# Graph passes with one comparison per group for the one-hots, and the edge weight applied on ScalarE

## What is computed

```python
# layer 0, per head; p = exp(leaky_relu(a_src[src] + a_dst[dst]) - max)
out = segment_sum(p[:, :, None] * h[src], dst)       # 256 columns + 4 of p
# layer 2
messages = edge_val[:, None] * embeddings[edge_src]
neighbor_emb = segment_sum(messages, edge_dst)       # 256 columns
```

## Time and profile before

| | |
|---|---|
| median of 3 runs | 9505.01 us (9503.06 to 9507.33) |
| profiled execution, first to last instruction | 9491.7 us |
| first graph pass, in the span | 187 to 2396 us |
| second graph pass, in the span | 3767 to 5880 us |
| busy: PE, DVE, ACT, POOL | 71%, 57%, 10%, 62% |
| mean granted clock of TensorE | 0.83 of full speed |

### The profile page before, as it was taken

How to read it: one execution, slowest core, us unless ns; L and a number is a source line. 1 busy time by engine, 2 the same in 40 slices (tenths; PEclk the granted TensorE clock), 3 DMA queues, 4 the chain that set the end, 5 groups by cost and what they waited for, 6 DMA issues and landing times. The chain is left out here.

```text
span 9491.7 us, 113426 instructions
## 1 busy us (share of the span) xinstructions
PE 6725.8 (71%) x23837; PEld 4472.8 (47%) x23838; DVE 5384.8 (57%) x13915; ACT 978.0 (10%) x2770; POOL 5926.5 (62%) x6521
## 2 busy tenths in 40 slices
PE   4777777777389992555555555677777777777893
PEld 3666666666256661444444444533333333333562
DVE  4777777777641114555555555566666666666422
ACT  1111111111033330000000000200000000000331
POOL 3777777777011115777777775077777777777125
PEclk7888888888599996777777777689999999999896
DMA  3333333333310003333333332100000000000113
GB/s 110 102 101 101 101 101 101 101 101 101 97 59 30 31 30 108 104 104 104 104 104 104 104 104 80 28 5 5 5 5 5 5 5 5 5 5 5 61 58 101
DMA packets 348160, 613.47 MB, mean 65 GB/s; under 512 B 123719, under 2 KB 223627, under 8 KB 348094
## 3 DMA queue, kind: packets, MB, share of 16 engines
q0 software_dynamic: 237632, 507.28, 21.1%
q1 hardware_dynamic: 110462, 105.48, 3.5%
HBM read 550.01 MB, written 62.36 MB: 65 GB/s over the span
## 5 line engine op out<-in xcount | busy, mean ns | idle before, releaser
L622 POOL DMA_INDIRECT g_G<-table,g_STG x3328 | 3254.4, 978 | 956.3 <-issue 887.7
L776 PE MATMUL g_pM<-g_G,g_S 128*128 128x260 f32 (+1 forms) x6656 | 2358.0, 519 | 1061.0 <-DMA g_G<-table,g_STG 1056.7
L776 PEld LDWEIGHTS g_pM<-g_G,g_S 128*128 128x128 f32 x6656 | 1665.5, 263 | 1575.0 <-issue 1112.0
L1355 PE MATMUL q_pS<-q_MV,q_OL 128*128 128x500 f32 (+1 forms) x4096 | 1966.7, 632 | 596.7 <-DVE q_MV L1251 596.7
L658 DVE TENSOR_TENSOR acc<-g_pM,acc 128x260 f32 (+1 forms) x3328 | 1407.5, 423 | 780.1 <-PE g_pM L776 757.8
L1355 PEld LDWEIGHTS q_pS<-q_MV,q_OL 128*128 128x128 f32 x4096 | 817.8, 207 | 1506.2 <-issue 841.0
L1162 POOL DMA_INDIRECT q_G<-table,q_STG x1024 | 1107.9, 1082 | 293.3 <-issue 293.3
L1251 DVE TENSOR_TENSOR q_MV<-q_OH,q_V 128x980 f32<-128x980 f32 x1024 | 1169.7, 1173 | 153.0 <-PE q_pS L1355 137.5
L1165 POOL DMA_INDIRECT q_A<-adst,q_STG x768 | 944.4, 1230 | 234.0 <-issue 233.4
L1690 POOL DMA_INDIRECT e_XI<-rows,e_STG x206 | 200.2, 972 | 1089.2 <-PE e_pI L1762 1086.0
L649 DVE TENSOR_SCALAR g_S<-iota,g_REL,g_WT 128x128 f32<-128x128 f32 x1664 | 617.9, 372 | 194.9 <-issue 178.3
(11 more groups left out here) (257 smaller groups left out, 4622.3 us busy)
## 6 DMA issues: line engine op xcount, KB each, us to landing
g_G<-table,g_STG POOLq DMA_INDIRECT x3328
ys<-e_Y SPq DMA_DIRECT2D x206, 128.0 KB, 1.7
ew_W<-in_L_ffn_W SPq DMA_DIRECT2D x16, 1024.0 KB, 9.2
q_G<-table,q_STG POOLq DMA_INDIRECT x1024
rows<-t_XR SPq DMA_DIRECT2D x98, 128.0 KB, 1.7
q_A<-adst,q_STG POOLq DMA_INDIRECT x768
table<-p_OUT SPq DMA_DIRECT2D x49, 130.0 KB, 1.9
f_H<-table SPq DMA_DIRECT2D x7, 896.0 KB, 4.8
```

Of the source, the lines that this page charges most:

```text
L622: pool.indirect_dma_start(G[:, r, u, :], None, table, bass.IndirectOffsetOnAxis(ap=STG[:, r, u:u + 1].bitcast(U32), axis=0)).then_inc(gath ...
L776: pe.matmul(pM[u % BANKS][:, 0:width], S[:, r, u, :], G[:, r, u, :], start=True, stop=True).then_inc(s["sum"], 1)
L1355: mm = pe.matmul(pS[j][:, 0:m * VC], OL[:, r, u, :], MV[:, u % MVR, b0:b0 + m, :].rearrange("p i c -> p (i c)"), start=(isinstance(k, int) ...
```

## The change

In both passes, the eight one-hots of a group are now made by one `tensor_tensor` that compares iota, broadcast over the eight tiles, with the group's eight columns of REL, broadcast over the 128 nodes: 1024 elements per partition, two inputs in SBUF. In the second pass the one-hots hold 1 and no longer the weight; ACT multiplies each tile of gathered rows by its column of WT, in place (one activation Copy with a per-partition scale, 128x256), and PE waits for that tile's scaling. In the first pass DVE's order changes: Z, add 0, ReLU, add 1, ARG, adds 2 and 3, then the one-hots of k+1, then L702 and adds 4 to 7 as before. PE's two half transposes both wait for the one instruction. In the second pass the one-hots of k+1 stand ahead of the eight adds of k.

```diff
--- before.py
+++ after.py
@@ -556,6 +556,8 @@
     names = ["loaded", "staged", "slots_free", "onehot", "sum", "added"]
     if attend:
         names += ["turned", "copied", "ad", "z", "lr", "arg", "p", "gp"]
+    else:
+        names += ["scaled"]
     s = {n: sh.sem(f"{tag}_{n}") for n in names}
     with Scope(nc) as sc:
         IDX = sc.sb(f"{tag}_IDX", [P, NS], I32)
@@ -636,18 +638,13 @@
             v.wait_ge(*acc_zeroed)
             regs = [v.alloc_register(f"{tag}_v{u}") for u in range(GRP)]
 
-            def onehot(rnd, r, u):
-
-                j = (rnd * RINGS + r) * GRP + u
-                rel = REL[:, bass.ds(j, 1)]
-                if u == 0:
-
-                    at_least(v, s["sum"], (rnd * RINGS + r - RINGS + 1) * GRP)
-                if attend:
-                    v.tensor_scalar(S[:, r, u, :], sh.iota[:, :], rel, None, ALU.is_equal).then_inc(s["onehot"], 1)
-                else:
-                    v.tensor_scalar(S[:, r, u, :], sh.iota[:, :], rel, WT[:, bass.ds(j, 1)],
-                                    ALU.is_equal, ALU.mult).then_inc(s["onehot"], 1)
+            def onehots(rnd, r):
+
+                k = rnd * RINGS + r
+                at_least(v, s["sum"], (k - RINGS + 1) * GRP)
+                v.tensor_tensor(S[:, r], sh.iota[:, :].unsqueeze(1).broadcast_to([P, GRP, P]),
+                                REL[:, bass.ds(k * GRP, GRP)].unsqueeze(2).broadcast_to([P, GRP, P]),
+                                ALU.is_equal).then_inc(s["onehot"], 1)
 
             def add(k, u, blk):
 
@@ -669,11 +666,6 @@
                 if before:
                     blk = load_registers(v, regs, BLK, (k - 1) * GRP)
 
-                def next_onehots(us):
-                    if not last(rnd, r):
-                        for u in us:
-                            onehot(*after(rnd, r), u)
-
                 def add_before(u):
                     if before:
                         add(k - 1, u, blk[u])
@@ -683,18 +675,18 @@
                 v.tensor_tensor(Z[:, par, 0], G[:, r, :, D:D + HEADS], pA[:, par], ALU.add).then_inc(s["z"], 1)
                 v.tensor_tensor(Z[:, par, 1], gmax[:, :].unsqueeze(1).broadcast_to([P, GRP, HEADS]), pA[:, par],
                                 ALU.add).then_inc(s["z"], 1)
-                next_onehots((0, 1))
-
+                add_before(0)
                 v.wait_ge(s["z"], k * 2 + 2)
                 v.scalar_tensor_tensor(L[:, par].rearrange("p a u h -> p (a u h)"), Z[:, par].rearrange("p a u h -> p (a u h)"),
                                        SLOPE, Z[:, par].rearrange("p a u h -> p (a u h)"),
                                        ALU.mult, ALU.max).then_inc(s["lr"], 1)
-                next_onehots((2, 3))
+                add_before(1)
                 v.wait_ge(s["lr"], k + 1)
                 v.tensor_tensor(ARG[:, par], L[:, par, 0], L[:, par, 1], ALU.subtract).then_inc(s["arg"], 1)
-                for u in range(HG):
+                for u in range(2, HG):
                     add_before(u)
-                    next_onehots((HG + u,))
+                if not last(rnd, r):
+                    onehots(*after(rnd, r))
                 v.wait_ge(s["p"], k + 1)
                 for q in range(HG):
                     rows = G[:, r, 2 * q:2 * q + 2, 0:D].rearrange("p u (h q) -> p u h q", h=HEADS)
@@ -704,13 +696,12 @@
 
             def step_weighted(rnd, r):
                 blk = load_registers(v, regs, BLK, (rnd * RINGS + r) * GRP)
+                if not last(rnd, r):
+                    onehots(*after(rnd, r))
                 for u in range(GRP):
-                    if not last(rnd, r):
-                        onehot(*after(rnd, r), u)
                     add(rnd * RINGS + r, u, blk[u])
 
-            for u in range(GRP):
-                onehot(0, 0, u)
+            onehots(0, 0)
             if attend:
                 over_groups(v, step_attend)
                 blk = load_registers(v, regs, BLK, (SG - 1) * GRP)
@@ -742,6 +733,19 @@
                 copy(0, 0)
                 copy(0, 1)
                 over_groups(a, step)
+        else:
+            @block.scalar
+            def _(a):
+                a.wait_ge(s["loaded"], n_loads)
+
+                def step(rnd, r):
+                    k = rnd * RINGS + r
+                    gathered(a, rnd, r)
+                    for u in range(GRP):
+                        a.activation(G[:, r, u, :], G[:, r, u, :], ACT.Copy,
+                                     scale=WT[:, bass.ds(k * GRP + u, 1)]).then_inc(s["scaled"], 1)
+
+                over_groups(a, step)
 
         @block.tensor
         def _(pe):
@@ -749,7 +753,7 @@
 
             def transposes(k, r, hf):
                 at_least(pe, s["copied"], 2 * k - 1 + hf)
-                pe.wait_ge(s["onehot"], k * GRP + (hf + 1) * HG)
+                pe.wait_ge(s["onehot"], k + 1)
                 for u in range(hf * HG, (hf + 1) * HG):
                     m = pe.transpose(pT[:, u, :], S[:, r, u, :], sh.ident[:, :])
                 m.then_inc(s["turned"], 1)
@@ -770,8 +774,10 @@
                     j = k * GRP + u
                     if attend and u % 2 == 0:
                         pe.wait_ge(s["gp"], k * HG + u // 2 + 1)
-                    if not attend and u == 0:
-                        pe.wait_ge(s["onehot"], (k + 1) * GRP)
+                    if not attend:
+                        if u == 0:
+                            pe.wait_ge(s["onehot"], k + 1)
+                        pe.wait_ge(s["scaled"], j + 1)
                     at_least(pe, s["added"], j + 1 - BANKS)
                     pe.matmul(pM[u % BANKS][:, 0:width], S[:, r, u, :], G[:, r, u, :], start=True,
                               stop=True).then_inc(s["sum"], 1)
@@ -788,7 +794,6 @@
                 sums(k, r, range(HG))
 
             def step_weighted(rnd, r):
-                gathered(pe, rnd, r)
                 sums(rnd * RINGS + r, r, range(GRP))
 
             pe.wait_ge(s["loaded"], n_loads)
```

## The result

The changed kernel takes 9654.72 us (median of 4 runs, 9649.76 to 9662.8) beside 9504.82 us before: a ratio of 1.0158, with a 95% interval from 1.0143 to 1.0172. It is slower by 150 us. The profiled execution has a span of 9648.0 us in place of 9491.7, 156 us more.

A forecast was written before the change was run, and what follows sets the result against it. POOL's line of gathers was taken to bound both graph passes: 9505 + 177 (second pass) + 177 (first pass) + 0 for ACT's scaling = 9859 us. The stated range was 9640 to 10000 us.

The forecast's parts named there:

- rival 2: Both passes: slower by little, 0.3 us a group in each, 9629 us; 20%.
- The mechanism and the sign: Both passes: DVE's operation with two SBUF inputs delays POOL's gathers, which set the time; slower, 91%.
- ACT's price: Second pass: eight scalings per group at 0.5 us each, hidden, costing 0 beyond the phase.
- The rule on the small comparisons: Both passes: SBUF-to-SBUF tensor_scalar in 2-port mode blocks GpSimd; removing eight would return 77 us per pass; doubted for the second.
- I take 0.85: Loss per group taken for each pass, 0.85 us, so 177 us per pass.
- The window was too wide: Gathers read indices 0.13 us after starting and wait out a running two-SBUF-input operation; 1.23 us comparison, mean delay 0.60 us.
- 0.85 by phase: Second pass: comparison starting at T + 10.7 to 11.4 delays copy or gather, 0.7 to 0.95 us a group.
- 0.60 taken: First pass: the comparison at Z + 2.54 might cost 0.13 or 1.1 us; unknown-phase mean 0.60 taken.
- 0.74 taken: First pass: four later multiplications cover gathers' readings, 0.74 us a group in place of today's 0.45.
- Slower by little: Both passes: kind phases in one or a copy that does not wait, 0.3 us a group each, 9629 us; 20%.
- The faster one: Both passes: comparison falls between readings and today's collisions vanish, floor 9400 us; 5%.
- bound of the first pass: First pass: PE becomes the bound at 12.2 us a group, costing 343 us, total 10025 us; 16%.

The follow-up runs named there:

- e3: Kernel before with only the second pass's weight moved to ACT, eight small comparisons still on DVE: 9502.3 us, ratio 1.0005.
- e4: Changed kernel with iota, one input of the comparison, in PSUM instead of SBUF: 9497.73 us, ratio 0.9997 to the kernel before.
- e9: Kernel before with only the factor p of the first pass's multiplications read from PSUM: 9416.34 us, ratio 0.9916; on chips with halts 10448.2 and 10358.23.
- e7: Changed kernel with iota and the first pass's factor p in PSUM: 9425.79 us, ratio 0.9926; on chips with halts 10522.33 to 10546.48.
- e8: e7 with the values V of the pass over the free edges also in PSUM: 11089.49 us, ratio 1.0567, only on a chip with halts.

## Why the prediction was wrong in size, and where it was right

The forecast was 9859 us, 354 over before; measured are 9655, 150 over. That 9655 still lies inside the stated range (9640 to 10000) is owed to the room left for rival 2 at its lower end and not to the forecast's own terms.

**The mechanism and the sign** were right. POOL's gathers set both passes; the operation of two SBUF inputs holds them off; ACT's part is free (e3). With one input in PSUM the loss is gone (e4). ACT's price was right too (0.5 us taken, 494 ns measured). The Trainium skill's sentence (SBUF — State Buffer, Who interferes with whom) on DVE instructions with two SBUF inputs holds here for gathers and for POOL's copy: 0.99 us with two, 0.19 with one.

**The rule on the small comparisons** as locks (the Trainium skill, same section) would have given back 77 us a pass by the prediction's estimate. The runs show far less. In the second pass the gathers take 950 ns with the eight (before) and 948 without them (e4). In the first pass the small comparisons do hold gathers, but little: e9 has them and no other such operation, and its gathers take 957 ns, where those of e7, without them, take 950. That is 13 us in the pass:

```profile
L623 POOL DMA_INDIRECT g_G<-table,g_STG x1664 | 1593.1, 957 | 478.2 <-issue 443.9 <-POOL g_STG L614 22.3 <-PE g_pM L778 12.1
...
L626 POOL DMA_INDIRECT g_G<-table,g_STG x1664 | 1580.1, 950 | 498.7 <-issue 481.1 <-PE g_pM L787 10.2 <-POOL g_STG L617 7.4
```

**The step that failed** is "I take 0.85", once for each pass. Measured are 0.54 and 0.22 us a group, so 112 and 45 us in place of 177 and 177.

- *The window was too wide.* I had a gather held whenever the operation ran 0.13 us after its start. The changed kernel's trace has many pairs: a gather that starts up to 0.03 us behind the comparison's start, or ahead of it, goes free; one from 0.05 us on is held until 0.13 us before the comparison's end (4598.20: 4599.33 - 0.13 - 4598.20 = 1.00, measured 1.97 - 0.97 = 1.00). So the window is about the length less 0.13: 1.10 us. The mean over phases is 1.10 x 1.10 / 2.5 = 0.48 and not 0.60, and that of the four multiplications 4 x 0.55 x 0.55 / 2.5 = 0.48 and not 0.74.
- *Second pass: 0.85 by phase.* I had narrowed the start to 0.7 us and reckoned two groups in turn. The starts in fact wander over more than one gather's distance (T + 10.5 to 12.7), partly since each delay moves the next group's phase. And the prediction read the two groups of the earlier trace rows as one at the higher clock and one not. In the trace the granted clock is at its lower level (0.50) when the matmuls of either begin; its mean is 0.92 from 3783 to 3785.5 in the one and 0.70 from 4611 to 4614 in the other, so neither group ran at one level. Cost: 0.54, near the mean over phases. Knowing the phase no better than this, that mean was the value to take.
- *First pass, the comparison: 0.60 taken, 0.27 measured.* Summed in the trace over 205 groups: gathers that start under it lose 56.0 us. Here my start was nearly right (Z + 2.54, median Z + 2.60), and the cost of 0.13 that I had worked out for it is nearer than the mean of an unknown phase, for which I gave it up.
- *First pass, the multiplications: 0.74 taken, 0.40 measured* (69.0 us on gathers and 13.3 on copies in 205 groups). They cost 0.39 before by the same count, so their moving by 1.66 us (from Z + 3.79 to Z + 5.45) changed next to nothing; in e4, with the same order, they cost 0.49. I compared a worked-out mean with a measured 0.45; the measured value for the same four operations was the better estimate of both.
- *The removed small comparisons* gave back 0.05 us a group in the first pass (11.1 us in 205 groups), which the prediction counted as the multiplications' in its 0.45.

With the corrected terms the first pass comes to 0.27 + 0.40 - 0.45 = 0.22, as measured.

**The rivals.** "Slower by little" (9629) was nearest, with two reasons, kind phases or a copy that does not wait. The first is the case in the first pass (0.22 where it had 0.3) and not in the second (0.54 where it had 0.3); the second is not, the copy waits like a gather. The faster one did not come. PE did not become the bound of the first pass on the chips where before takes 9500 us: the multiplications start as worked out, and e4 has all of PE's later work with a first pass of (2383.3 - 185.5) / 1663 x 8 = 10.57 us a group.

**What stays open.** e7 should have been 10 us faster than e9 and is 9 us slower. Its gathers are shorter by 13 us in the first pass, by the two rows above, but POOL stands idle 499 us ahead of them in place of 478. The trace shows some of that in 36 waits of 0.4 to 1.9 us, which come back every 246 us and make 16 us; their cause is open. So is that of the common halts, of POOL's waits for PE on those chips, and of DVE's standing still in e8.

## What to carry to other kernels

When POOL's gathers set the time, look at every DVE operation longer than a few tenths of a microsecond and count its SBUF inputs: one input in PSUM costs DVE nothing here and frees the gathers. Then time the whole kernel: in e8 the gathers became short and the kernel 5.7% slower than before. Merging eight short operations into one long one saved DVE 1.0 and 1.7 us of busy time a group and cost POOL 0.2 and 0.5. For an operation that comes once per group at a phase that you can't hold, reckon with window x window / (2 x distance), and where the trace has a measured value for the same operations, take that one on both sides of the difference.

## What the runs showed of the hardware that I had not expected

- The hold ends 0.13 us before the profile's end of the DVE operation for a gather and 0.15 for a copy, and does not touch a gather that starts with it: a free gap of 0.15 us where I had reckoned 0.02.
- A multiplication of 128x512 with a broadcast factor takes 677 ns with the factor in PSUM and 682 with it in SBUF; the comparison of 1024 takes 1.22 us either way.
- The activation of 128x256 in SBUF with a per-partition scale has a mean of 494 ns, and eight in a row take 3.30 us, 0.41 each.
- The kernel before takes 9500 us on some chips and 10480 to 10543 on three others. With e9, traced on both kinds, 990 of 1037 us more lie in the two passes full of gathers, in waits of POOL; 387 us of them are 255 stretches in which all engines stand still.
